# A sandwich layer with windowed attention on one core: q and k rows stored lane by head, loaded by half slots in 16 transfers, with signals per half slot

## The chip, the cores and the metric

The kernel runs on one core of a Trainium2 chip. The metric is the device time of one execution in microseconds (us), lower is better. TensorE, VectorE, ScalarE, GpSimd and SyncE are the engines of the core; SyncE (SP) does no arithmetic here, it issues DMA transfers one after the other from its queue, and 16 DMA engines carry them out.

## What is computed

x has 2 sequences of 2048 tokens with 128 features. The layer is, cut to what matters (all in float32, LN without gain):

```python
x = x + LN(attn(LN(x)))          # this part holds the change
x = x + LN(ffn(LN(x)))           # 4 experts, argmax routing, exact gelu; not touched

def attn(x):
    q, k, v = split(x @ qkv_w + qkv_b, 3)         # 16 heads of 8
    # head by head: position t sees positions t-128 .. t-1
    local = softmax(mask(q k^T / sqrt(8))) v
    # 64 pooled tokens per sequence, 4 heads of 8, earlier chunks only
    remote = (softmax(mask(rq rk^T / sqrt(8))) rv) @ rout_w + rout_b
    gate = sigmoid(local @ gl_w + remote_h @ gr_w)
    return (gate * local + (1 - gate) * remote_h) @ out_w + out_b
```

## The kernel before, in words

The work has three stages, each a block of programs for the five engines; all engines must have finished a stage before the next one begins: `project`, `attend` and `ffn`. The order on every engine is written out by hand (a function `emit` per engine, called for each chunk or step), and semaphores tie the engines together. A `Signal` is a semaphore with a count per step.

**project** runs over 8 chunks of 512 tokens. Per chunk: statistics and normalisation (VectorE, with GpSimd for the root), transposes (TensorE), copies (ScalarE, line 626), then the products q, k, v and rq (TensorE, lines 685 to 697). q and k are wanted at more than bfloat16 precision, so each is split in three bfloat16 parts whose sum it is: ScalarE writes the high part (line 633), VectorE the residue (line 527), ScalarE the middle part (line 643), GpSimd the low part (line 593). SyncE stores the parts to DRAM (`store`, lines 444 to 455): q_parts and k_parts, three transfers each, then v_tok and rq_t. The tiles `split`, `vt` and `rqs` have two buffers, so ScalarE's high part of chunk c waits on `s_out` for the stores of chunk c-2.

In DRAM q_parts and k_parts have the shape [part, chunk, d, head, token]. The partitions of the product are (head, d), and the store turns that round.

**The load.** In attention a product of q and k is one matmul over 48 rows: six of the nine products of parts, each over 8 rows d. Therefore `qst` holds the parts of q as row blocks 0,1,2 = part 0 three times, 3,4 = part 1 twice, 5 = part 2, and `kst` holds parts 0,1,2, then 0,1, then 0 of k. Both have two slots; a slot holds one chunk (4 blocks of 128 tokens, 16 heads). The slot is loaded in 4 groups of 4 heads, with three transfers for q and three for k in each (`load_q`, `load_k`, lines 222 to 237):

```python
RUNS = ((0, 3), (3, 2), (5, 1))
src = scratch[0][part, c, :, heads]...           # [8, 4 * 512]
sp.dma_start(dst, src.unsqueeze(0).broadcast_to([times, HD, HG * CH]))
src = scratch[1][0:parts, c, :, heads]...        # [parts, 8, 4 * 512]
```

`load_rest` adds vst (from v_tok) and rqT (from rq_t). All 26 transfers of a slot count on one semaphore, `s_load[slot]`.

**When the loads are issued.** Chunk 0 is loaded in `project`, by `first_blocks`: groups 0 and 1 behind the store of chunk 4, groups 2 and 3 with vst and rqT behind the store of chunk 5. Chunk 1 is loaded at the very start of `attend`. Chunk c from 2 on is loaded in steps 4(c-1) (q) and 4(c-1)+1 (k, then vst and rqT); `paced` holds SyncE until TensorE has got to a named unit of the transposed scores (`s_ST`), since the slot is still being read.

**attend** runs over steps s of one block of 128 tokens, with 8 units g of two heads per step. TensorE makes in unit g the scores of block s+2 (`scores`, lines 930 to 936), for VectorE to take the row maxima (line 1088), and the transposed scores of block s (`scores_t`, lines 948 to 967), for ScalarE's exponentials (line 1291), then products with v (line 981). The negated maxima of a block are split by GpSimd (line 1226), transposed by TensorE, copied by ScalarE (line 1303) to `mT` and written by a DMA (SyncE, line 895, "the maxima's transfer") into two further rows of `qst`; block s+1's go out in the middle of step s and `scores_t` of block s+1 waits for them. The wait for a slot stands on TensorE in front of unit 0 of the scores of its first block:

```python
if g == 0 and n.mod(LC) == 0:      # n = s + 2, in step s = 4c - 2
    pe.wait_ge(s_load[c % SLOTS], 16 * LOADS * (c // SLOTS + 1))
```

At its start `attend` has VectorE clear three PSUM banks and fill small tiles (lines 1072 to 1076), and TensorE waits for that (`s_consts`).

## Time and profile before

| what | us |
| --- | --- |
| median of 3 runs | 685.05 |
| lowest and highest run | 683.4 and 690.52 |
| the profiled execution | 687.44 |
| its span (first to last instruction) | 685.6 |
| project, until SyncE's first issue of attend | 94.2 |
| attend, until TensorE's last work in it | about 504 |

A profile shows one execution. "Busy" is time in which an engine worked on an instruction; a matmul's end is modelled. A wait is put down to what came last. PE is TensorE's matmuls, PEld its weight loads, DVE VectorE, ACT ScalarE, POOL GpSimd, SPq SyncE's queue. The clock is the share of full speed that TensorE was granted, 1.00 or 0.50 at any time. The DMA share is the mean busy share of the 16 DMA engines.

### The profile page before, as it was taken

How to read it: one execution, taken by the hardware profiler on the slowest of the kernel's cores; microseconds unless marked ns; L12 is line 12 of the kernel's file. 1: busy time of each engine (PE TensorE's matmuls, PEld its weight loads, DVE VectorE, ACT ScalarE, POOL GpSimd, SP SyncE). 2: the span in 40 equal slices, each digit the busy share in tenths (PEclk: the TensorE clock that was granted, in tenths of full speed). 3: DMA queues.
4: the chain of work that ended last, by engine and by line, in shares of the span. 5: the costliest groups of instructions: out<-in, count | busy, mean ns of one | idle time of the engine just before them, and what ended most of it. 6: DMA issues, size and time to landing. Idle time of an engine off the chain costs nothing. (4 is left out here: it accounts for less than half of the span.)

```text
span 685.6 us, 28265 instructions
## 1 busy us (share of the span) xinstructions
PE 558.6 (81%) x11345; PEld 391.0 (57%) x11345; DVE 407.7 (59%) x2034; ACT 288.9 (42%) x787; POOL 238.4 (35%) x465
## 2 busy tenths in 40 slices
PE   7887545979599598697685895898789999999992
PEld 3544212757477376475564674676536777667772
DVE  6684424557367386276464465477656467667655
ACT  2353200657367376276464464487512221221110
POOL 5545100134235243153243233245531243342342
PEclk9999867799799799599799698599999999999998
DMA  3474532111202102002002012000000000000001
GB/s 77 133 212 154 173 111 83 41 61 44 78 6 64 58 13 78 36 22 90 15 28 90 8 32 88 5 6 6 3 0 1 1 2 15 15 15 16 17 15 31
DMA packets 28506, 33.30 MB, mean 49 GB/s; under 512 B 5852, under 2 KB 22212, under 8 KB 28380
## 3 DMA queue, kind: packets, MB, share of 16 engines
q1 hardware_dynamic: 27324, 31.20, 14.6%
q8 instruction: 88, 1.44, 0.9%
q10 hardware_dynamic: 1056, 0.35, 0.2%
q14 instruction: 38, 0.31, 0.2%
HBM read 19.93 MB, written 11.27 MB: 46 GB/s over the span
## 5 line engine op out<-in xcount | busy, mean ns | idle before, releaser
L1088 DVE CUSTOM_DVE_ANT_0 added<-psS,maskq 128x160 bf16<-128x160 f32 x512 | 157.1, 316 | 147.6 <-PE psS L936 87.9
L1291 ACT ACTIVATE probs<-psST 128x512 f32<-128x512 f32 x256 | 152.7, 604 | 157.1 <-PE psST L967 154.3
L967 PE MATMUL psST<-qst,kst 98*32 98x128 bf16 (+3 forms) x2048 | 86.9, 207 | 5.6 <-issue 5.4
L981 PE MATMUL psPV<-probs,vst 128*9 128x128 f32 x1984 | 88.0, 289 | 2.2 <-issue 2.2
L963 PE MATMUL psST<-qst,kst 98*32 98x32 bf16 (+3 forms) x1920 | 83.6, 207 | 5.1 <-issue 5.0
L1263 POOL TENSOR_TENSOR gated<-both,glr 128x256 f32<-128x256 f32 x32 | 23.5, 733 | 143.0 <-DVE both L1189 143.0
L933 PE MATMUL psS<-kst,qst 68*32 68x96 bf16 (+3 forms) x512 | 24.3, 231 | 57.7 <-DMA rqT<-rq_t 48.8
L1724 ACT ACTIVATE hT<-fpsH 128x512 f32<-128x512 f32 x32 | 19.1, 598 | 121.6 <-PE fpsH L1468 121.6
L930 PE MATMUL psS<-kst,qst 68*32 68x160 bf16 x1536 | 67.0, 241 | 3.3 <-issue 2.3
L963 PEld LDWEIGHTS psST<-qst,kst 98*32 98x32 bf16 x1920 | 60.2, 101 | 6.5 <-issue 6.5
L951 PE MATMUL psST<-maskk,identb 128*32 128x128 bf16 x960 | 60.9, 231 | 0.3 <-issue 0.3
L967 PEld LDWEIGHTS psST<-qst,kst 98*32 98x32 bf16 x2048 | 55.9, 103 | 6.6 <-issue 6.3
L933 PEld LDWEIGHTS psS<-kst,qst 68*32 68x32 bf16 x512 | 14.8, 110 | 74.7 <-DMA rqT<-rq_t 50.5
L1465 PE MATMUL fpsH<-xehi,w1hi 128*128 128x512 f32 x128 | 55.7, 435 | 0.0
L981 PEld LDWEIGHTS psPV<-probs,vst 128*9 128x9 f32 x1984 | 49.9, 94 | 4.6 <-issue 3.2
L1465 PE MATMUL fpsH<-xelo,w1hi 128*128 128x512 f32 x128 | 50.6, 395 | 0.0
L1465 PE MATMUL fpsH<-xehi,w1lo 128*128 128x512 f32 x128 | 50.5, 395 | 0.0
L930 PEld LDWEIGHTS psS<-kst,qst 68*32 68x32 bf16 x1536 | 31.6, 96 | 30.7 <-issue 15.4
L1088 DVE DVE_READ_ACCUMULATOR2_ANT rowmax<- 128x1 f32 x512 | 42.1, 82 | 0.1
L1325 ACT ACTIVATE lexp<-psA,lbias 128x64 f32<-128x64 f32 x128 | 39.8, 328 | 0.0
L1644 DVE TENSOR_TENSOR xehi<-fpsE,xfThi 128x512 fp32r<-128x512 f32 x32 | 22.0, 688 | 17.5 <-PE fpsE L1476 9.7
L951 PEld LDWEIGHTS psST<-maskk,identb 128*32 128x32 bf16 x960 | 29.6, 101 | 4.4 <-ACT probs L1291 2.3
(183 smaller groups left out, 1237.7 us busy)
## 6 DMA issues: line engine op xcount, KB each, us to landing
q_parts<-split SPq DMA_DIRECT2D x24, 128.0 KB, 2.7
k_parts<-split SPq DMA_DIRECT2D x24, 128.0 KB, 2.7
qst<-q_parts SPq DMA_DIRECT2D x32, 96.0 KB
kst<-k_parts SPq DMA_DIRECT2D x32, 96.0 KB
v_tok<-vt SPq DMA_DIRECT2D x8, 288.0 KB, 2.6
vst<-v_tok SPq DMA_DIRECT2D x8, 288.0 KB
X<-in_L_attn_x_dram SPq DMA_DIRECT2D x8, 256.0 KB, 3.2
qst<-q_parts SPq DMA_DIRECT2D x32, 64.0 KB
```

The lines of the kernel that those rows point to most:

```text
L930: last = nc.tensor.matmul(bank[quad(i), a, 0:WIN], q, part(kst, KPROD, n - 1, h, QD * i, WIN), start=True, stop=True)
L933: nc.tensor.matmul(bank[quad(i), a, 0:P - QD * i], q, part(kst, KPROD, n - (1 if n.k else 0), h, QD * i, P - QD * i), start=True, stop=True)
L951: nc.tensor.matmul(bank[quad(j)].rearrange("p a (s q) -> p a s q", s=2)[:, :, :, quad(j)], pick, maskk[:].unsqueeze(1).broadcast_to([P, 2, ...
L963: nc.tensor.matmul(bank[quad(j), a, 0:QD * (j + 1)], part(kst, KALL, n - 1, h, QD * j, QD), part(qst, KALL, n, h, 0, QD * (j + 1)), start= ...
L967: last = nc.tensor.matmul(bank[quad(j), a, P + QD * j:2 * P], part(kst, KALL, n, h, QD * j, QD), part(qst, KALL, n, h, QD * j, P - QD * j) ...
L981: last = nc.tensor.matmul(psPV[32 * t:32 * t + VW, G * P:(G + 1) * P], vst[:, (n - 1 + side).mod(RING), 4 * G + t, :], probs[:, unit, (2 * ...
L1088: taken = nc.vector.tensor_tensor_reduce(added[:, h], psS[g % 2][:, a, 0:WIN], mask, 1.0, NEG * 4, ALU.add, ALU.max, rowmax[:, n.mod(2), h ...
L1263: nc.gpsimd.tensor_tensor(gated[:].rearrange("p h (a e) -> p a h e", a=2), both[:, n.mod(4)].rearrange("p a (h e) -> p a h e", h=H), glr[: ...
L1291: nc.scalar.activation(probs[:, g], psST[g % 2][:].rearrange("p a c -> p (a c)"), ACT.Exp, scale=SCALE).then_inc(s_exp.sem, 1)
L1325: nc.scalar.activation(lexp[:, h], psLS[:, h * NLAT:(h + 1) * NLAT], ACT.Exp, bias=lbias[:, s.mod(2), h:h + 1], scale=SCALE, accum_out=lsu ...
L1465: nc.tensor.matmul(psH[j % 2][:], w[:, e, tile], x[:, u, e], start=(e == 0 and k == 0), stop=False)
L1644: nc.vector.tensor_tensor(xehi[:, u, e], psE[e % 2][:], xfThi[:, u].bitcast(F32), ALU.mult)
```

## The change

Four things change.

1. *Lane by head.* ScalarE copies the q and k weights once into `wqk` with reordered columns, before chunk 0, and the biases are read in the same order; TensorE waits for the two copies (`s_lanes`). The partitions of the products are then (d, head), and the DRAM tensors become [chunk, part, (d, head), token]. The three parts of q are one store, and those of k another: 4 stores per chunk in place of 8.
2. *Fewer and larger loads.* A slot is loaded in two halves of 8 heads, each with three transfers for q and four for k, with vst and rqT: 16 in place of 26. The row of a head group is contiguous, 8 heads x 512 x 2 bytes = 8 KB, in place of 4 KB, and source and destination are plain matrices. In k the six blocks hold other parts (0, 1, 0, 1, 1, 2); with q's (0, 1, 2, 0, 1, 0) they give the same six products.
3. *Signals.* `s_half[half][slot]` replaces `s_load`: TensorE waits for half 0 in front of unit 0 and for half 1 in front of unit 4 of the scores, and for vst and rqT (`s_rest`) only two steps later, in front of `scores_t` of the first block. The wait for `s_consts` moves there too, in step 0.
4. *Places.* Chunk 1 is now loaded in `project` as well, behind the stores of chunks 6 and 7. In attention, step 4(c-1) issues half 0 (q at its start, k after unit 4 of the transposed scores), and the next step half 1 with vst and rqT.

```diff
-HG = 4
-STORES = 16 * 8
-LOADS = 6 * H // HG + 2
-RUNS = ((0, 3), (3, 2), (5, 1))
+HALF = H // 2
+STORES = 16 * 4
+RUNS_Q = ((0, 0, 3), (3, 0, 2), (5, 0, 1))
+RUNS_K = ((0, 0, 1), (1, 0, 1), (2, 0, 2), (4, 1, 2))
+LOADS = 16 * (len(RUNS_Q) + len(RUNS_K))
...
+def load_half(sp, c, half, side, held, scratch, s_half):
+
+    u, heads = c % SLOTS, slice(half * HALF, (half + 1) * HALF)
+    tile, runs = ((held.qst, RUNS_Q), (held.kst, RUNS_K))[side]
+    rows = scratch[side][c].rearrange("a (d h) t -> (a d) h t", h=H)[:, heads].rearrange("r h t -> r (h t)")
+    for first, part, parts in runs:
+        sp.dma_start(tile[first * HD:(first + parts) * HD, u, heads].rearrange("r h t -> r (h t)"),
+                     rows[part * HD:(part + parts) * HD]).then_inc(s_half[half][u], 16)
...
-        q_parts = nc.dram_tensor("q_parts", [3, NCH, HD, H, CH], BF16, kind="Internal").ap()
+        q_parts = nc.dram_tensor("q_parts", [NCH, 3, P, CH], BF16, kind="Internal").ap()
...
-                    for part in range(3):
-                        sp.dma_start(parts[part, c.k].rearrange("d h t -> h d t"),
-                                     split[:, u, side, part]).then_inc(s_out[u], 16)
+                    sp.dma_start(parts[c.k].rearrange("a p t -> p a t"), split[:, u, side]).then_inc(s_out[u], 16)
...
-                for hg in range(2 * k, 2 * k + 2) if k < 2 else ():
-                    load_q(sp, 0, hg, held, scratch, s_load)
-                    load_k(sp, 0, hg, held, scratch, s_load)
-                if k == 1:
-                    load_rest(sp, 0, held, scratch, s_load)
+                for side in range(2):
+                    load_half(sp, k // 2, k % 2, side, held, scratch, s_half)
+                if k % 2:
+                    load_rest(sp, k // 2, held, scratch, s_rest)
...
+            for side in range(2):
+                nc.scalar.activation(wqk[:, side].rearrange("k (d h) -> k d h", h=H),
+                                     wqkv[:, side * D:(side + 1) * D].rearrange("k (h d) -> k d h", h=H),
+                                     ACT.Copy).then_inc(s_lanes, 1)
...
+                half = s.mod(LC) if s.live and 2 <= c < NCH and s.mod(LC) < 2 else None
+                if half is not None:
+                    sp.wait_ge(s_ST.sem, s_ST.after(s - 1))
+                    load_half(sp, c, half, 0, held, scratch, s_half)
...
+                if half is not None:
+                    if half == 0:
+                        sp.wait_ge(s_ST.sem, s_ST.after(s, HALF // 2))
+                    load_half(sp, c, half, 1, held, scratch, s_half)
+                if half == 1:
                     sp.wait_ge(s_pv.sem, s_pv.after(s - 1))
-                    paced(s, 5)
-                    load_rest(sp, c, held, scratch, s_load)
+                    load_rest(sp, c, held, scratch, s_rest)
...
-            pe.wait_ge(s_consts, CONSTS)
...
-                        if g == 0 and n.mod(LC) == 0:
+                        if g % (HALF // 2) == 0 and n.mod(LC) == 0:
                             c = n.k // LC
-                            pe.wait_ge(s_load[c % SLOTS], 16 * LOADS * (c // SLOTS + 1))
+                            pe.wait_ge(s_half[2 * g // HALF][c % SLOTS], LOADS * (c // SLOTS + 1))
```

SyncE's queue at the end of `project`, before: the stores of chunk 7 (and the last of chunk 6's), the end of the stage, and the first issues of `attend`. An operand such as 24x1x2048 is the shape of the transfer, x2 a repetition.

```order
L451 DMA v_tok<-vt 128x576 [waits s_vt]
L455 DMA rq_t<-rqs 32x512 [waits s_rqs]
L479 DMA kst<-ones 2x16x512 [waits s_clear_late]
L479 DMA kst<-ones 2x16x512
L448 DMA q_parts<-split 16x8x512 [waits s_lo]
L448 DMA q_parts<-split 16x8x512 x2
L448 DMA k_parts<-split 16x8x512 [waits s_lo]
L448 DMA k_parts<-split 16x8x512 x2
L451 DMA v_tok<-vt 128x576 [waits s_vt]
L455 DMA rq_t<-rqs 32x512 [waits s_rqs]
L317 UNCONDITIONAL_BRANCH [waits s_out1,s_out0,s_ones]
L869 UNCONDITIONAL_BRANCH [waits barrier_Pool_Activation_PE_DVE_SP_release]
```

The same place now, from the stores of chunk 7 on: its loads of chunk 1's second half stand between the stores and the end of the stage.

```order
L443 DMA q_parts<-split 128x3x512 [waits s_lo]
L443 DMA k_parts<-split 128x3x512 [waits s_lo]
L445 DMA v_tok<-vt 128x576 [waits s_vt]
L449 DMA rq_t<-rqs 32x512 [waits s_rqs]
L229 DMA qst<-q_parts 24x4096
L229 DMA qst<-q_parts 16x4096
L229 DMA qst<-q_parts 8x4096
L229 DMA kst<-k_parts 8x4096 x2
L229 DMA kst<-k_parts 16x4096 x2
L237 DMA vst<-v_tok 128x576
L239 DMA rqT<-rq_t 32x512
L311 UNCONDITIONAL_BRANCH [waits s_out1,s_out0,s_ones]
```

The stage ends behind 16 issues less of stores (4 per chunk over chunks 4 to 7) and 6 more of loads.

SyncE's queue in attention, steps 4 and the start of 5 (chunk 2), before; `qst<-mT` is the maxima's transfer.

```order
L895 DMA qst<-mT 2x16x128 [waits s_mTc]
L228 DMA qst<-q_parts 24x1x2048 [waits s_ST]
L228 DMA qst<-q_parts 16x1x2048
L228 DMA qst<-q_parts 8x2048
L228 DMA qst<-q_parts 24x1x2048
L228 DMA qst<-q_parts 16x1x2048
L228 DMA qst<-q_parts 8x2048
L895 DMA qst<-mT 2x16x128 [waits s_mTc]
L228 DMA qst<-q_parts 24x1x2048 [waits s_ST]
L228 DMA qst<-q_parts 16x1x2048
L228 DMA qst<-q_parts 8x2048
```

The same steps now, with the start of step 5:

```order
L878 DMA qst<-mT 2x16x128 [waits s_mTc]
L229 DMA qst<-q_parts 24x4096 [waits s_ST]
L229 DMA qst<-q_parts 16x4096
L229 DMA qst<-q_parts 8x4096
L878 DMA qst<-mT 2x16x128 [waits s_mTc]
L229 DMA kst<-k_parts 8x4096 [waits s_ST]
L229 DMA kst<-k_parts 8x4096
L229 DMA kst<-k_parts 16x4096 x2
L229 DMA qst<-q_parts 24x4096 [waits s_ST]
L229 DMA qst<-q_parts 16x4096
L229 DMA qst<-q_parts 8x4096
L878 DMA qst<-mT 2x16x128 [waits s_mTc]
```

In step 4 stand now 3 issues of q and 4 of k where 12 of q stood; k no longer waits for step 5, and q's second half does.

## Rows read from the trace of the kernel before

**Rows 1.** The page: span, busy time by engine, and granted clock and DMA in 40 slices

```profile
span 685.6 us, 28265 instructions
...
PE 558.6 (81%) x11345; PEld 391.0 (57%) x11345; DVE 407.7 (59%) x2034; ACT 288.9 (42%) x787; POOL 238.4 (35%) x465
...
PEclk9999867799799799599799698599999999999998
DMA  3474532111202102002002012000000000000001
```

**Rows 2.** The list of waits: engine and line, who was waited for, total us, times, longest

```profile
ACT probs L1291 <- PE psST L967: 154.3, 130, 11.7
...
PE psS L933 <- DMA rqT<-rq_t: 48.8, 6, 8.8
...
ACT split L633 <- DMA rq_t<-rqs: 17.5, 5, 7.0
...
PE psST L948 <- DMA qst<-mT: 8.2, 1, 8.2
```

**Rows 3.** The timeline of SyncE's queue, 206 to 227 us: start, us, what, count

```profile
206.59 3.78 SPq L228 DMA_DIRECT2D qst<-q_parts  x6
...
221.56 3.75 SPq L237 DMA_DIRECT2D kst<-k_parts  x6
225.42 0.36 SPq L244 DMA_DIRECT2D vst<-v_tok  x1
225.82 0.42 SPq L246 DMA_DIRECT2D rqT<-rq_t  x1
```

**Rows 4.** Stretches of the DMA tail: us, busy times, clock, DMA share, GB/s

```profile
226.00:228.00 2.00, 0.00 (x0) 0.00 (x0) 0.27 (x3) 0.00 (x0) 0.66 (x3) 1.00 0.71 214
228.00:232.00 4.00, 0.00 (x0) 0.00 (x0) 0.00 (x0) 0.00 (x0) 0.00 (x0) 0.59 0.14 53
```

**Rows 5.** Stretches between every fourth copy of the maxima: first, last, and the sum of six

```profile
142.80:191.20 48.40, 37.84 (x1284) 28.80 (x1283) 27.84 (x181) 27.55 (x85) 17.23 (x43) 0.89 0.17 52
...
383.60:435.00 51.40, 40.12 (x1286) 30.26 (x1285) 28.54 (x184) 28.20 (x86) 17.61 (x44) 0.80 0.13 42
sum 292.20, PE 226.89 PEld 173.92 DVE 168.74 ACT 166.56 POOL 105.41; mean PE 37.82 PEld 28.99 DVE 28.12 ACT 27.76 POOL 17.57
```

**Rows 6.** Single steps as stretches, and one fall of the clock

```profile
174.10:177.50 3.40, 3.40 (x77) 2.19 (x69) 1.76 (x11) 1.55 (x6) 0.00 (x0) 0.50 0.22 77
201.30:209.80 8.50, 8.47 (x307) 6.60 (x305) 6.86 (x46) 6.78 (x23) 3.41 (x10) 1.00 0.08 21
435.00:447.40 12.40, 12.40 (x349) 9.31 (x347) 6.70 (x46) 7.10 (x23) 3.55 (x9) 0.65 0.01 3
```

**Rows 7.** The timeline at the start of attention: VectorE, ScalarE, TensorE

```profile
95.56 0.48 DVE L1072 MEMSET psPV<- 128x512 f32 x1 [11.09 <-issue]
...
98.12 0.32 DVE L1088 CUSTOM_DVE_ANT_0 added<-psS,maskq 128x160 bf16<-128x160 f32 x1 [0.74 <-PE psS L936]
...
109.36 0.27 ACT L1303 ACTIVATE mT<-psB 32x128 bf16<-32x128 bf16 x1 [32.00 <-PE psB L1016]
...
120.59 0.41 PE L948 MATMUL psST<-never,identb 128*32 128x256 bf16 x4 [8.22 <-DMA qst<-mT]
```

**Rows 8.** The timeline of SyncE's queue at the end of the projection stage

```profile
51.71 1.85 SPq L448 DMA_DIRECT2D q_parts<-split  x3
...
56.74 2.25 SPq L228 DMA_DIRECT2D qst<-q_parts  x3
...
89.88 0.38 SPq L455 DMA_DIRECT2D rq_t<-rqs  x1
```

**Rows 9.** The timeline of ScalarE and TensorE in the projection stage

```profile
12.98 0.60 ACT L626 ACTIVATE xnT<-psT 128x512 f32<-128x512 f32 x1 [6.55 <-PE psT L674]
...
73.76 0.69 ACT L633 ACTIVATE split<-psQ,bq 128x512 bf16<-128x512 f32 x1 [6.99 <-DMA rq_t<-rqs]
...
82.95 5.57 PE L122 MATMUL psW<-filler 128*128 128x512 bf16 x25
```

More of the change, by code:

```diff
@@ L219, in apply, with load_rest @@
         last.then_inc(self.s_xf.sem, 1)
[L222 to L240 removed]
+def load_half(sp, c, half, side, held, scratch, s_half):
[5 more added lines that the diff above has]
+                     rows[part * HD:(part + parts) * HD]).then_inc(s_half[half][u], 16)
+def load_rest(sp, c, held, scratch, s_rest):
     _, _, v_tok, rq_t = scratch
@@ L276, in sandwich @@
         norm = InputNorm(nc, sb, lambda name: ctx.enter_context(nc.semaphore(name)), X, eps_col, mhalf)
-        s_load = [ctx.enter_context(nc.semaphore(f"s_load{r}")) for r in range(SLOTS)]
+        s_half = [[ctx.enter_context(nc.semaphore(f"s_half{j}{r}")) for r in range(SLOTS)] for j in range(2)]
+        s_rest = [ctx.enter_context(nc.semaphore(f"s_rest{r}")) for r in range(SLOTS)]
         until_attend = ctx.enter_context(ExitStack())
@@ L397, in project @@
         s_prep = sem("s_prep")
+        s_lanes = sem("s_lanes")
         s_lat = sem("s_lat")
@@ L667, in _ @@
             pe.wait_ge(s_w, all_weights)
+            pe.wait_ge(s_lanes, 2)
             def transpose(c):
```

70 lines of the change are left out of this document (19 added, 51 removed).

## The prediction

> **What bounds the kernel now.** I read four views, in this order. The page first [rows 1]: over the whole span TensorE is busy 81%, more than any other engine, yet in the middle slices (the attention stage) the row of granted clock falls from 9 to 7 or less at regular distances. The DMA engines are busy 1 or 2 tenths there, so their bandwidth as a whole is not used up.
>
> The list of waits says why [rows 2]. TensorE waited six times, 48.8 us in all, for the last transfer of the next slot's load (rqT) and once 8.2 us for the row of maxima (qst from mT). ScalarE waited 17.5 us in five pieces for stores in the projection stage. ScalarE's long wait (154 us) is a wait for the matmuls: it shows that TensorE leads, and costs nothing.
>
> Third, SyncE and the DMA engines at one of the six places [rows 3, 4]. SyncE issues the 24 q and k transfers of a slot at 0.62 us each (3.75 us for six), the last at 225.8 us, and TensorE has stood still since 225.5 us, because it waits for the whole slot at the first unit of step 4c-2. After the last issue the DMA engines are busy 0.14 of 16, that is 2.2 engines, at 53 GB/s, until the load has landed at about 233.7 us. Two engines hold a queue and fourteen are empty. One of the two moves 53/2.2 = 24 GB/s, so a 4 KB row takes about 0.17 us.
>
> Fourth, the stretches [rows 5, 6]. I cut the trace at every fourth copy of the maxima (ScalarE's line 1303). Six such periods of four blocks take 292.2 us with TensorE busy 226.9 us. A step of one block in a quiet place at full clock takes 8.50 us, busy 8.47: there TensorE alone sets the pace.
>
> **The load.** How the rows fall on engines is my reading of the operands. A slot has 8 groups (4 head groups, q and k) of three transfers. The sources count 3 copies or parts, then 2, then 8 rows in front. If that front count is the number of engines used, the two lowest engines get 8 + 8 + 1 = 17 rows of 4 KB per group, 136 of the slot's 384; at 0.17 us that is 23 us. This agrees with two engines still busy 8 us after SyncE's last issue, with the first issue at 206.6 us [rows 3, 4]. The Trainium skill, "DMA: Bandwidth & Descriptors", section "Why a DMA increments its semaphore by 16 and not by 1", says it directly: the engines used are the largest number up to 16 that divides the slowest dimension (not 1) of source and destination, taken from the lowest. By that rule the trace agrees, at 2.2 engines.
>
> After the change a transfer is a plain matrix of 24, 16 or 8 rows of 8 KB. If all rows count, the busiest engine gets 2 + 1 + 1 rows of q and 1 + 1 + 1 + 1 of k per half, 16 rows per slot, 16 x 0.34 = 5.4 us in place of 23. If instead they stay on two engines, half the bytes are about 23 us again; both ends are kept, and I take the first, as the 2.2 engines fit that reading and no other I can think of.
>
> The time at which they are needed moves too. The q half and the k half of heads 8 to 15 are issued in step 4c-3 (7 issues, at most 0.62 us each, 4.3 us), and needed at the fifth unit of step 4c-2; vst and rqT are needed two blocks later than before. That is over 8.5 us after the issue [rows 6]: the six waits go, 48.8 us.
>
> **The clock.** After each stall the granted clock is at its lower level (1.2 GHz in place of 2.4) while work goes on. A step mostly at the lower level has 349 matmuls in 12.40 us, the quiet one 307 in 8.50 [rows 6]. With a mean clock of 0.65, 8.7 us of it are at the half level and 3.7 at the full one; those 3.7 take 134 matmuls at 28 ns, which leaves 215 in 8.7 us, 40 ns each: 0.3 of such time is lost. From the mean clocks of the six periods (0.89, 0.90, 0.90, 0.81, 0.91, 0.80) 77 us are at the half level [rows 5]; The clock falls some 3.3 us into a stall (228 to 232 us has a mean of 0.59, so it fell at 228.7 [rows 4]), so 48.8 - 6 x 3.3 = 29 of the 77 lie in the stalls themselves and 48 in work: 15 us lost. So a period's matmul work at full clock is (226.9 - 15)/6 = 35.3 us, and its idle time beside the stall (292.2 - 226.9 - 48.8)/6 = 2.75: 38.0 us. I put 0.6 on top for clock falls that follow no stall. 6 x 38.6 = 231.6: **60.6 us gained**, stalls and clock together. If the clock did not recover it would be 12 less, if it never fell 4 more. The step after the sixth period takes 12.4 us; its 349 matmuls at 28 ns are 9.8, with 0.3 idle 10.1 [rows 6]: **2.3**.
>
> **Start of attention.** Now slot 1 is loaded there: 26 issues are 16 us of SyncE's queue, from 94.2 to 110.7, and keep the two engines until about 120. The maxima of block 0 were copied at 109.36, and their transfer (2 rows in front, so the same two engines) lands at 120.5 [rows 7]: **8.2 us gained**, as these loads are issued before. The half clock behind it costs less afterwards, **1.5**. That TensorE no longer waits for the memsets gives the first unit of scores, 0.7 us (VectorE's first maximum waited 0.74 [rows 7]): **0.7**, since VectorE's own start does not move.
>
> **Projection stage.** From 51.7 us SyncE issues without a gap: four groups of stores (8 issues, 5.0 us each), 12 loads (7.9), 14 loads (8.8), two rows of ones (1.4), and gaps: 38.5 us until 90.26 [rows 8]. Then it waits for the last store (2.6) and all engines leave the stage: it is the last, TensorE had ended at 88.5 [rows 9]. Afterwards a store group is 4 issues, 0.62 + 0.62 + 0.6 + 0.37 = 2.2 us; the loads are 7 + 9 + 7 + 9 issues, although 16 of them are new here. A two-dimensional transfer costs 0.36 (vst) or 0.42 (rqT), a three-dimensional one 0.62 [rows 3]; I take 0.44 for 28 of them and 0.8 for each pair of vst and rqT: 14. Sum 8.8 + 14 + 1.4 = 24 us (at 0.62: 29). The last stores are followed by 9 loads, so their landing is covered. ScalarE's high parts waited five times, 17.5 us, for stores of two chunks before [rows 2]; the last one, chunk 7's, 6.99 us, was chunk 5's store behind 12 load issues [rows 8, 9]. From high part to landed store I count 10.5 to 11.5 us per two chunks, so chunk 7's comes at about 59.5 us in place of 73.8, and TensorE's end 14.7 us behind it, at 74.2. SyncE's chain, begun at 48, ends at 72 to 77. The stage ends at about 75.9 in place of 92.9: **17.0 us gained**. Lower bound 9 (issue time alone, at 0.62), upper bound 19.
>
> Added: two copies of 128 x 128 on ScalarE before chunk 0. ScalarE sat idle 6.55 us before its first copy, at 12.98 us, while TensorE ran fillers [rows 9]: nothing, with that cover gone 0.6 us. The reordered bias is 128 runs of 4 bytes, as before. The feed-forward stage (190 us) is not touched.
>
> **Sum.** 60.6 + 2.3 + 8.2 + 1.5 + 0.7 + 17.0 = 90.3 us. The profiled execution took 687.4 (span 685.6 and 1.8 around it): 597.1. It lay 2.4 above the median of the runs (685.05): **595 us**.
>
> **Rivals.**
> - The clock stays as it is. For it: the trace has falls of the clock that no stall precedes, as at 174.1 us [rows 6]. Then the 15 us are not won back, and the projection gives 13 instead of 17: 595 + 14 + 4 = 613.
> - The rows still gather on two engines (a front count is not what decides). The slot's 23 us fit into a period of 38, so the long wait still goes, but each of 12 steps with loads has the maxima's transfer behind 8 KB rows on those two engines, 2 to 4 us late: 36 us. About 631. Against it: nothing else explains 2.2 engines.
> - Slower: plain matrices land on one engine. 192 rows of 8 KB at 0.34 us are 65 us per slot. From 38.6 us per slot on, the load sets the period, and at 48.7 the gain is gone; at 65 the six periods take 98 us more than before, about 685 - 28 + 98 = 755. Against it: when vst and rqT, plain matrices too, are under way, the share of busy engines is 0.71, at 214 GB/s [rows 4].
> - The loads moved into the projection are what ends it: 32 loads at 0.62 us and stores that wait for them, the stage ends at 84: 603. That is inside the range.
>
> Chances: forecast 0.64, clock 0.2, two engines 0.09, the longer projection 0.05, one engine 0.02. The range takes in the bounds of projection and clock: 580 (2 better in the projection, periods of 37.5 us, and 3 us at the start of attention if the clock is up there) to 618. Faster by over 1%, which is about what a measurement of this kernel can tell from no change: 0.97; within 1%: 0.01; slower: 0.02.
>
> **What the profile after would show.** The wait for rqT is gone, and none of over 1 us for a half slot stands in its place. Periods of four blocks take 38 to 39 us, with a clock over 0.95. After SyncE's last issue of a slot the DMA share falls within 2 or 3 us, not 8. TensorE's wait for the maxima at the start of attention is under 1 us. VectorE's memset of psPV starts at 77 to 80 us in place of 95.56. The prediction is wrong if the periods stay over 42 us with gaps on TensorE, if SyncE is at the stage's end after 84 us, or if load issues cost over 0.62 us.

## The result, and the profile after

| what | before, us | after, us |
| --- | --- | --- |
| median of 4 runs each | 684.64 | 637.99 |
| lowest and highest run | 683.4 and 690.52 | 630.17 and 643.61 |
| the profiled execution | 687.44 | 643.61 |
| its span | 685.6 | 641.8 |

The ratio is 0.9265, 95% interval 0.9159 to 0.937: the change made the kernel 47 us faster, where 90 were forecast (595 us, range 580 to 618). The profiled execution is the longest and slowest of the four runs, 5.6 us above their median, so what is read from its trace is too long by up to as much.

One slip in the section on the change: the six row blocks of k hold the parts (0, 0, 0, 1, 1, 2), as `RUNS_K` in the diff says, and not (0, 1, 0, 1, 1, 2). No time hangs on it.

The page after:

```profile
span 641.8 us, 28150 instructions
...
PE 556.4 (87%) x11337; PEld 391.6 (61%) x11345; DVE 407.5 (63%) x2034; ACT 290.3 (45%) x789; POOL 238.1 (37%) x465
...
PEclk9898959889796999996988987998999999999997
DMA  3478930214212224043032142000000000000001
...
q1 hardware_dynamic: 25788, 31.20, 21.0%
q8 instruction: 88, 1.44, 1.0%
```

Beside [rows 1] TensorE's busy time is almost the same (558.6 before), so nearly all of the gain is idle time that went. The clock row still has holes, and the middle slices of the DMA row are higher. q1 carries the data, q8 is a queue of its own that brings instructions: 88 packets, 1.44 MB, 16 KB each. The prediction did not count with it.

TensorE's waits within the six periods, copies of the maxima 4 to 28 (engine, line, what ended the wait, total us, times, longest):

```profile
PE psST L940 <- issue: 9.3, 7, 1.8
PE psST L944 <- issue: 8.8, 6, 3.4
PE psPV L958 <- issue: 5.0, 6, 2.1
PE psST L928 <- issue: 4.7, 3, 1.9
```

The six waits for rqT of [rows 2] (48.8 us) are gone, and no wait for a half slot stands here. What stands here ends with "issue", with nothing that the profile can name: 22 pauses and 27.8 us in these four rows, 32.3 us with the smaller ones, of 35.0 us of idle time. The same sum is 15.4 us in the six periods of the kernel before.

The six periods, and the step after them, as stretches (us, then busy of PE, PEld, DVE, ACT, POOL, clock, DMA share, GB/s):

```profile
125.90:171.30 45.40, 40.65 (x1288) 30.79 (x1286) 27.38 (x178) 27.72 (x85) 16.46 (x42) 0.85 0.29 55
...
347.10:391.80 44.70, 38.25 (x1288) 29.35 (x1286) 28.86 (x185) 27.80 (x86) 17.52 (x44) 0.91 0.28 48
sum 265.90, PE 230.94 PEld 177.59 DVE 168.56 ACT 166.74 POOL 105.27; mean PE 38.49 PEld 29.60 DVE 28.09 ACT 27.79 POOL 17.54
...
391.80:403.10 11.30, 11.30 (x347) 8.51 (x345) 6.61 (x44) 7.14 (x23) 3.56 (x10) 0.70 0.03 5
```

Against [rows 5] the six take 265.9 us in place of 292.2: TensorE's idle time falls from 65.3 to 35.0 us, but its busy time rises from 226.9 to 230.9. The clock is 0.90 on average, not over 0.95: by its records TensorE was at the lower level for 54.8 us of the six periods (76.6 before). Every fall there stands behind a pause of TensorE of 0.9 us or more.

The start of attention, on VectorE, ScalarE and TensorE, against [rows 7]:

```profile
88.81 0.48 DVE L1054 MEMSET psPV<- 128x512 f32 x1 [14.35 <-issue]
...
90.86 0.33 DVE L1070 CUSTOM_DVE_ANT_0 added<-psS,maskq 128x160 bf16<-128x160 f32 x1 [0.23 <-DVE psST L1058]
...
101.56 0.27 ACT L1285 ACTIVATE mT<-psB 32x128 bf16<-32x128 bf16 x1 [31.46 <-PE psB L998]
...
104.48 0.29 PE L925 MATMUL psST<-never,identb 128*32 128x256 bf16 x4
```

The first transposed scores follow the copy of the maxima by 2.9 us (11.2 before), without a wait for their transfer. But the memset that opens the stage comes at 88.81, not at 78.5. The end of the projection stage says why, first SyncE's queue, then stretches:

```profile
74.14 0.90 SPq L449 DMA_DIRECT2D rq_t<-rqs  x1
75.08 1.45 SPq L229 DMA_DIRECT2D qst<-q_parts  x3
76.58 1.46 SPq L229 DMA_DIRECT2D kst<-k_parts  x4
...
78.54 0.43 SPq L239 DMA_DIRECT2D rqT<-rq_t  x1
```

```profile
76.00:78.00 2.00, 2.00 (x10) 0.94 (x10) 0.00 (x0) 0.00 (x0) 0.00 (x0) 1.00 1.09 286
...
80.00:82.00 2.00, 0.00 (x0) 0.00 (x0) 0.00 (x0) 0.00 (x0) 0.00 (x0) 0.93 1.12 198
82.00:84.00 2.00, 0.00 (x0) 0.00 (x0) 0.00 (x0) 0.00 (x0) 0.00 (x0) 0.50 0.72 138
84.00:86.00 2.00, 0.00 (x0) 0.00 (x0) 0.00 (x0) 0.00 (x0) 0.00 (x0) 0.50 0.54 164
```

SyncE has issued all at 78.97 us, 2 us after the forecast's 72 to 77, and then waits 7.9 us for the last store (rq_t). All 16 DMA engines are full until 82 (a share over 1 is overlap in the records) and still have work at 86; TensorE does nothing from 78.5 to 89.1 us. So the stage waits for bytes, not for issues.

Where the 43.8 us between the two profiled executions come from, by the terms of the prediction:

| term | forecast | measured |
| --- | --- | --- |
| six periods | 60.6 | 26.3 |
| projection, until the memset of psPV | 17.0 | 6.75 |
| from there to the fourth copy of the maxima | 10.4 | 10.2 |
| from the 28th copy to TensorE's last matmul in attention | 2.3 | 0.8 |
| sum | 90.3 | 44.0 |

### The profile page after: what moved, and what is told of

The parts are those of the page before. It is cut to its first block and busy times, and to the rows that moved or that the text cites. A ratio compares the mean times of both kernels' runs of the same rounds, so it can differ in the third digit from the quotient of the medians.

```text
span 641.8 us, 28150 instructions
## 1 busy us (share of the span) xinstructions
PE 556.4 (87%) x11337; PEld 391.6 (61%) x11345; DVE 407.5 (63%) x2034; ACT 290.3 (45%) x789; POOL 238.1 (37%) x465
## 3 DMA queue, kind: packets, MB, share of 16 engines
q1 hardware_dynamic: 25788, 31.20, 21.0%
q8 instruction: 88, 1.44, 1.0%
## 5 line engine op out<-in xcount | busy, mean ns | idle before, releaser
L944 PE MATMUL psST<-qst,kst 98*32 98x64 bf16 (+3 forms) x2048 | 86.6, 206 | 9.2 <-issue 9.1
L958 PE MATMUL psPV<-probs,vst 128*9 128x128 f32 x1984 | 90.0, 292 | 5.0 <-issue 5.0
L928 PE MATMUL psST<-maskk,identb 128*32 128x128 bf16 x960 | 62.2, 234 | 5.8 <-issue 4.7
L907 PEld LDWEIGHTS psS<-kst,qst 68*32 68x32 bf16 x1536 | 30.8, 97 | 33.0 <-issue 17.3
L910 PE MATMUL psS<-kst,qst 68*32 68x96 bf16 (+3 forms) x512 | 23.0, 217 | 10.9 <-issue 10.9
L1447 PEld LDWEIGHTS fpsH<-xehi,w1hi 128*128 128x128 f32 x128 | 24.0, 188 | 11.9 <-issue 8.4
```

What stands on the lines that cost most here:

```text
L907: last = nc.tensor.matmul(bank[quad(i), a, 0:WIN], q, part(kst, KPROD, n - 1, h, QD * i, WIN), start=True, stop=True)
L910: nc.tensor.matmul(bank[quad(i), a, 0:P - QD * i], q, part(kst, KPROD, n - (1 if n.k else 0), h, QD * i, P - QD * i), start=True, stop=True)
L928: nc.tensor.matmul(bank[quad(j)].rearrange("p a (s q) -> p a s q", s=2)[:, :, :, quad(j)], pick, maskk[:].unsqueeze(1).broadcast_to([P, 2, ...
L944: last = nc.tensor.matmul(bank[quad(j), a, P + QD * j:2 * P], part(kst, KALL, n, h, QD * j, QD), part(qst, KALL, n, h, QD * j, P - QD * j) ...
L958: last = nc.tensor.matmul(psPV[32 * t:32 * t + VW, G * P:(G + 1) * P], vst[:, (n - 1 + side).mod(RING), 4 * G + t, :], probs[:, unit, (2 * ...
L1447: nc.tensor.matmul(psH[j % 2][:], w[:, e, tile], x[:, u, e], start=(e == 0 and k == 0), stop=False)
```

## What the pauses are

In a trace read instruction by instruction, the pauses of TensorE have a pattern that no view prints. I counted TensorE's instructions (matmuls, weight loads, and the waits and other instructions of its sequencer) in the order of their records and cut them into pieces of 256. The number of the instruction that follows a pause of 0.6 us or more in the six periods, less a fixed offset, modulo 256:

```
before     0 or 1 (13 pauses, 0.6 to 1.2 us); 165, 210, 255, 172, 217, 6 (the waits for rqT)
after      0, 1 or 2 (23 of 23 pauses, 0.6 to 3.4 us)
a_noload   0, 1 or 2 (17 of 17 pauses, 0.7 to 1.8 us; an experiment, below)
```

So every pause of this length that is no wait for data stands at a cut. In the kernel after it ends 1.3 to 1.9 us after the end of a packet on q8, and a packet of 16 KB for 256 instructions is 64 bytes for each. A packet starts on average 1.30 us after TensorE has crossed the cut before, and takes 1.25 (without loads 1.13 and 1.13). With 1.4 us from its end to the next instruction that is some 3.9 us for 256 instructions (3.7 without loads). TensorE crosses a cut every 3.88 us in the middle (median of a_noload; some come after 2.8): it has almost no slack against the arrival of its own program, and had little before the change either.

Two of these pauses of the kernel after, with the load issues before them (TensorE, SyncE, then stretches):

```profile
154.72 0.23 PE L940 MATMUL psST<-qst,kst 98*32 98x96 bf16 x2 [1.36 <-issue]
...
368.82 0.24 PE L944 MATMUL psST<-qst,kst 98*32 98x96 bf16 x3 [3.39 <-issue]
```

```profile
148.50 1.42 SPq L229 DMA_DIRECT2D kst<-k_parts  x4
...
363.05 1.05 SPq L229 DMA_DIRECT2D qst<-q_parts  x3
```

```profile
145.00:147.00 2.00, 2.00 (x79) 1.73 (x78) 1.60 (x12) 1.80 (x4) 1.70 (x6) 1.00 0.83 127
...
149.00:151.00 2.00, 1.38 (x38) 0.97 (x38) 0.80 (x6) 0.29 (x2) 0.00 (x0) 1.00 0.80 164
...
153.00:155.00 2.00, 0.64 (x36) 0.49 (x39) 1.61 (x10) 0.74 (x3) 1.38 (x4) 1.00 0.00 0
...
363.00:365.00 2.00, 2.00 (x98) 1.65 (x94) 2.00 (x15) 1.87 (x6) 1.23 (x5) 1.00 0.67 135
365.00:367.00 2.00, 0.43 (x29) 0.28 (x22) 1.40 (x10) 0.28 (x1) 1.70 (x5) 1.00 0.45 66
367.00:369.00 2.00, 0.18 (x4) 0.18 (x3) 0.00 (x0) 0.00 (x0) 0.16 (x1) 0.86 0.03 4
```

A burst of loads occupies 13 of 16 engines (share 0.83) at 127 GB/s; TensorE pauses some microseconds later, when the DMA engines are idle again (0.00, 0.03) and nothing is being waited for. From this I formed the theory that the experiments test: **the load rows, now on nearly all engines, hold up the packets that bring TensorE its instructions; it pauses at the next cut, and the clock falls to its lower level for a while.** The rivals: the pauses are TensorE's waits for the half slots, put down wrongly; or they belong to the instruction stream alone and would be there without loads.

The Trainium skill, "Runtime: NRT & Kernel Launch", section "Instruction fetch mechanics", says that an engine fetches its program in blocks of 16 KiB, 256 instructions, over a DMA queue of its own, and calls the cost mostly hidden. The blocks and the queue are in this trace; hidden they are not: 32.3 us of pauses in 265.9.

## The experiments

Each ran beside the kernel before on the same chip. "Six" is the sum of the six periods in the profiled execution, "busy" and "idle" TensorE's in it; ratios are to the kernel before.

| kernel | median, us | ratio, 95% | six | busy | idle |
| --- | --- | --- | --- | --- | --- |
| after | 637.99 | 0.9265 (0.9159 to 0.937) | 265.9 | 230.9 | 35.0 |
| a_noload | 612.13 | 0.8923 (0.8869 to 0.8978) | 234.9 | 213.2 | 21.7 |
| b_dump | 632.85 | 0.92 (0.9123 to 0.9277) | 258.0 | 224.0 | 34.0 |
| a_two | 656.53 | 0.9587 (0.9515 to 0.9659) | 258.6 | 229.6 | 29.0 |
| a_whole | 640.7 | 0.9291 (0.9217 to 0.9365) | 267.7 | 229.8 | 37.9 |
| a_attend | 635.39 | 0.9265 (0.9208 to 0.9322) | 265.1 | 228.6 | 36.5 |
| a_wide | 623.65 | 0.9059 (0.9017 to 0.91) | 250.0 | 219.6 | 30.4 |
| a_eight | 624.57 | 0.9079 (0.903 to 0.9128) | 254.2 | 221.4 | 32.8 |
| a_quarter | 620.02 | 0.9009 (0.8967 to 0.905) | 247.6 | 220.5 | 27.1 |
| a_paced | 626.52 | 0.9086 (0.9038 to 0.9133) | 246.7 | 217.6 | 29.1 |
| b_qa | 611.62 | 0.891 (0.8853 to 0.8967) | 245.9 | 223.0 | 22.9 |
| b_qp | 622.63 | 0.9077 (0.9017 to 0.9137) | 248.6 | 222.8 | 25.8 |
| b_qap | 620.49 | 0.9035 (0.8982 to 0.9088) | 246.1 | 219.2 | 26.9 |

"Six", "busy" and "idle" come from one execution each. The kernel after and a_attend have the same loads in attention and almost the same six periods, 265.9 and 265.1 us, though a_attend's execution took 8.8 us less.

**No loads in attention (a_noload).** TensorE waits only for the first load of each slot, and blocks 8 to 31 are computed from the rows of chunks 0 and 1.

```diff
-                half = s.mod(LC) if s.live and 2 <= c < NCH and s.mod(LC) < 2 else None
+                half = None
...
-                            pe.wait_ge(s_half[2 * g // HALF][c % SLOTS], LOADS * (c // SLOTS + 1))
+                            pe.wait_ge(s_half[2 * g // HALF][c % SLOTS], LOADS)
...
-                            pe.wait_ge(s_rest[c % SLOTS], 16 * 2 * (c // SLOTS + 1))
+                            pe.wait_ge(s_rest[c % SLOTS], 16 * 2)
```

> The changed kernel without the slot loads of chunks 2 to 7 in attention (and without their three waits), so those blocks are computed from the data of chunks 0 and 1. Theory 1 (instruction supply): in the trace of the changed kernel every pause of TensorE put down to issue ends about 1.4 us behind a 16 KB instruction packet, and the long ones lie where load rows hold the DMA engines. Then these long pauses go, but the floor of about 3.9 us per instruction block stays: six periods of four blocks take 246 to 252 us in place of 266, time about 621. Theory 2 (clock and dependences, loads have no part in it): 634 to 642 as the changed kernel. The forecast's own picture (only the loads keep a period from 38.6 us): six periods in 232, time about 603.

Measured: 612.13 us. Two periods and the sum of the six:

```profile
124.50:164.40 39.90, 38.54 (x1287) 29.43 (x1286) 27.39 (x180) 27.54 (x86) 16.66 (x42) 0.88 0.06 14
164.40:203.20 38.80, 34.86 (x1285) 27.09 (x1284) 28.45 (x184) 27.68 (x86) 17.65 (x45) 1.00 0.02 6
...
sum 234.90, PE 213.20 PEld 165.14 DVE 168.19 ACT 165.66 POOL 105.07; mean PE 35.53 PEld 27.52 DVE 28.03 ACT 27.61 POOL 17.51
```

The floor is lower than I then thought, and almost what the prediction had computed: 39.15 us a period in place of 38.6, with 35.5 of matmul work in place of 35.3, at a clock of 1.00 in four of the six periods. So the prediction's arithmetic of a period was right for a kernel whose loads cost nothing, and the loads cost 31.0 us in these two executions (25.9 in the medians): 13.3 of idle time and 17.7 of longer matmuls. The matmuls are longer by the clock, which was at its lower level for 13.2 us here and 54.8 in the kernel after. Where it stays at 1.00, loads make no difference to them: the last period of a_paced, with loads, has TensorE busy 35.33 us, and the last one here 35.09.

**The same traffic into a tile that nobody reads (b_dump).** As a_noload, but with the loads of q and k.

```diff
+        dump = sb("dump", [6 * HD, 2, HALF, CH], BF16)
...
+                sp.dma_start(dump[first * HD:(first + parts) * HD, side].rearrange("r h t -> r (h t)"),
+                             rows[part * HD:(part + parts) * HD]).then_inc(s_dump, 16)
...
-                    load_half(sp, c, half, 0, held, scratch, s_half)
+                    load_dump(sp, c, half, 0)
```

> No step waits for a load, but the traffic stays: the q and k transfers of chunks 2 to 7 go, with the same shapes and at the same places, into a tile that nobody reads (vst and rqT of those chunks are left out, and blocks 8 to 31 are computed from the rows of chunks 0 and 1). Theory 1 (the load rows hold up the transfers that bring TensorE its instructions, so traffic alone costs the time): the six periods take about 258 to 266 us as with the real loads, and the time is 630 to 638 us. Theory 2 (what costs time is that TensorE depends on the loads, by its waits for the halves): the time is that of the kernel without loads, about 612 us, with periods of 235 us in sum.

```profile
sum 258.00, PE 223.98 PEld 172.87 DVE 169.17 ACT 166.84 POOL 105.35; mean PE 37.33 PEld 28.81 DVE 28.19 ACT 27.81 POOL 17.56
```

Measured: 632.85 us, and the six periods are at 258.0. Nothing on TensorE depends on these transfers, yet 23.1 of the 31.0 us are there (20.7 of 25.9 in the medians), and the waits put down to "issue" are 29.3 us, against 16.8 without loads and 32.3 in the kernel after. The traffic costs the time, not the waits. The other 8 us are left between the missing vst and rqT, the waits for them, and the scatter of single executions.

**All of a slot awaited at its first unit (a_whole).** The change's signals for the loads undone; the wait for `s_consts` stays where the change put it.

```diff
-                            pe.wait_ge(s_half[2 * g // HALF][c % SLOTS], LOADS * (c // SLOTS + 1))
+                            for j in range(2):
+                                pe.wait_ge(s_half[j][c % SLOTS], LOADS * (c // SLOTS + 1))
+                            pe.wait_ge(s_rest[c % SLOTS], 16 * 2 * (c // SLOTS + 1))
```

> The changed kernel with the half signals undone: TensorE waits for both halves and for vst and rqT in front of the first unit of a slot. If the spread loads land within 3 us of their last issue (theory of the forecast), no wait over 1 us stands there and the time is that of the changed kernel, 634 to 642. Rival (the half signals are what removed the wait): waits of 2 to 5 us at six places, 650 to 665.

```profile
PE psS L910 <- DMA rqT<-rq_t: 10.9, 4, 3.2
```

Measured: 640.7 us. The wait for rqT is back, four times and 10.9 us, in place of six times and 48.8 [rows 2]. I had expected none over 1 us. The six periods grow by only 1.8 us; that such a wait for data covers a pause that the program's arrival would have caused anyway is not shown. The signals per half are worth too little to tell from the scatter; the larger and better spread transfers took the long waits away.

**Rows gathered on two engines (a_two).** Each part plane gets 16 rows of padding in DRAM, so that parts and rows stay two dimensions, and a transfer has 3 or 2 in front.

```diff
-        q_parts = nc.dram_tensor("q_parts", [NCH, 3, P, CH], BF16, kind="Internal").ap()
+        q_parts = nc.dram_tensor("q_parts", [NCH, 3, P + H, CH], BF16, kind="Internal").ap()
...
-                     rows[part * HD:(part + parts) * HD]).then_inc(s_half[half][u], 16)
+                     rows[part:part + parts]).then_inc(s_half[half][u], 16)
```

> The changed kernel with part planes set apart in DRAM, so that the 24-row and 16-row loads keep 3 and 2 in front, as before the change. Bytes, row length, places and signals are those of the changed kernel. If the front count sets the number of DMA engines, the share after a slot's last issue is again about 0.13 for 10 us and more. Theory 1: the instruction packets mostly find free engines, the long issue pauses go, periods take 41 to 43 us in place of 44.4; but the projection stage ends later than 87 us, since stores queue behind loads on two engines; sum 625 to 640. Rival: the maxima's transfers, which go through the same two engines, are late in the 12 load steps: periods over 46 us and a wait for the maxima on TensorE of 10 us or more in all.

Its waits, and a stretch of a load:

```profile
PE psST L928 <- DMA qst<-mT: 17.9, 7, 4.1
...
PE psST L940 <- issue: 5.7, 6, 2.7
PE psST L944 <- issue: 3.4, 5, 0.9
```

```profile
164.00:166.00 2.00, 2.00 (x50) 1.35 (x44) 1.59 (x12) 1.67 (x4) 1.70 (x6) 1.00 0.24 78
```

Measured: 656.53 us. The share of busy engines in a load is 0.24 where it was 0.83, so the count in front of a transfer does decide how many engines carry it. The time is over the 625 to 640 us of the first theory, since what the rival names, late maxima, came on top. The psPV memset comes at 108.32 us, and the maxima's transfer is awaited seven times, 17.9 us. But the pauses of the kind "issue" shrink (in the six periods from 32.3 to 9.7 us), and the six periods are 7.3 us shorter than with all engines. An 8 KB row takes 311 ns here (median of the records) and 643 ns in the kernel after.

**Chunk 1 at the start of attention (a_attend).** The place of the loads undone, with 16 issues in place of 26.

```diff
-                for side in range(2):
-                    load_half(sp, k // 2, k % 2, side, held, scratch, s_half)
+                for side in range(2) if k < 2 else ():
+                    load_half(sp, 0, k % 2, side, held, scratch, s_half)
...
+            for half in range(2):
+                for side in range(2):
+                    load_half(sp, 1, half, side, held, scratch, s_half)
+            load_rest(sp, 1, held, scratch, s_rest)
```

> The changed kernel with chunk 1 loaded at the start of attention again (16 issues). Theory: in the changed kernel the end of the projection stage is set by the last stores, which queue behind 8 KB rows of chunk 1 on all 16 DMA engines (SyncE waited 7.9 us for them). Then VectorE's first memset of attention comes at 80 to 83 us in place of 88.8, the maxima's first transfer is not late (under 1 us of wait on TensorE), and the time is 630 to 633. Rival: the backlog only moves into attention: the transfer of block 0's maxima waits again 3 us or more and the time stays at 636 to 640.

VectorE, and the wait for the maxima on TensorE:

```profile
77.96 0.48 DVE L1059 MEMSET psPV<- 128x512 f32 x1 [5.94 <-issue]
...
95.29 0.41 PE L930 MATMUL psST<-never,identb 128*32 128x256 bf16 x4 [3.95 <-DMA qst<-mT]
```

Measured: 635.39 us. The memset comes at 77.96, within the 77 to 80 that the prediction named: the 17 us of the projection are there as soon as chunk 1's loads are not. Of the 10.9 us gained at the memset 8.5 are left at the fourth copy of the maxima (117.37 against 125.87), as part is paid back in a wait of 3.95 us for the maxima. The ratio is the same as the kernel after's, 0.9265: in the medians the gain is 2.6 us, less than their scatter. So the earlier end of the stage is shown, a shorter kernel by it is not; of the two expectations the rival, a wait of 3 us or more for the maxima, came nearer.

**Other shapes of the same bytes.** a_wide: one transfer of 48 rows per half and side, into every second partition (0 to 94), so that the products are made of other rows than the reference's. a_eight: every transfer has 8 rows, 12 per half. a_quarter: every transfer cut in two of 4 heads, 28 per slot with rows of 4 KB. a_paced: one transfer per unit of the transposed scores instead of three or four in a row.

```diff
# a_wide
+        sp.dma_start(tile[0:96:2, u, heads].rearrange("r h t -> r (h t)"),
+                     rows).then_inc(s_half[half][u], 16)
# a_eight
-RUNS_Q = ((0, 0, 3), (3, 0, 2), (5, 0, 1))
-RUNS_K = ((0, 0, 1), (1, 0, 1), (2, 0, 2), (4, 1, 2))
+RUNS_Q = tuple((i, part, 1) for i, part in enumerate((0, 1, 2, 0, 1, 0)))
+RUNS_K = tuple((i, part, 1) for i, part in enumerate((0, 0, 0, 1, 1, 2)))
# a_quarter
+    for heads in (slice((2 * half + j) * 4, (2 * half + j + 1) * 4) for j in range(2)):
...
# a_paced
+                    load_half(sp, c, half, 0, held, scratch, s_half,
+                              lambda i: sp.wait_ge(s_ST.sem, s_ST.after(s, i)) if i else None)
...
```

> The changed kernel with other loads for chunks 2 to 7 in attention: per half and side one transfer of 48 rows of 8 KB into every second partition from 0 to 94, in place of rows gathered in partitions 0 to 47. Bytes and row length are the same; those chunks are computed from wrong rows. Without loads six periods took 234.9 us, with them 265.9. Theory 1a (rows from 8 to 16 engines crowd into few partitions, so each row holds its engine twice as long, 9.6 GB/s per engine in place of 24, and TensorE's instruction packets wait behind them): the rate in a load's stretch rises from about 130 GB/s at a share of 0.83 to over 220 GB/s, the long pauses shrink, periods take 40.5 to 42 us in place of 44.3, time 618 to 626. Theory 1b (any burst on all engines delays the packets, whatever the rows' rate): 43.5 to 45, time as the changed kernel.

> The changed kernel with every q and k load as a transfer of one block, 8 rows of 8 KB: 12 in a half in place of 7. By the front count they use 8 engines. Theory 1: if the instruction packets run on an engine outside the lowest eight, the long pauses go and periods take 40 to 42 us; if inside, or if the rows' slow writing is what counts, 44 to 46. At the projection's end 10 issues more per pair of halves: VectorE's first memset of attention 90 to 95 us. Sum 625 to 645.

> The changed kernel with each transfer cut in two of 4 heads, rows of 4 KB (28 in place of 14 per slot), same engines, bytes and signals. Theory 1 with packets: an instruction packet waits behind whole rows on its engine, so half the row, half the wait: pauses from late packets (fetch start over 2 us behind the last one) from 6 to 2 or fewer, periods 42 to 43 us. Rival (it is the burst's length that counts, not the row): 44 to 45. The projection's end is as in the changed kernel, within 3 us, since the same bytes stand there.

> The changed kernel with the loads of attention spread over a step: one transfer per unit (q's three at units 0, 1, 2, k's four at units 4 to 7), in place of three and four in one burst. Same rows, bytes and engines. Theory 1: each burst is 0.5 to 1.5 us in place of 2 to 4, so no instruction packet waits over 1.5 us; the pauses over 1.5 us (14.6 us over six periods) go, and with them most falls of the clock: periods 41 to 42.5 us, time 620 to 630. Rival: the delay is spread over more packets and the sum stays: 44 us, 636 to 640.

Measured: 623.65, 624.57, 620.02 and 626.52 us. All four are faster than the kernel after, with intervals clear of its own, but not of one another. a_quarter has the lowest median, with its six periods at

```profile
sum 247.60, PE 220.51 PEld 170.79 DVE 168.79 ACT 166.11 POOL 105.02; mean PE 36.75 PEld 28.47 DVE 28.13 ACT 27.68 POOL 17.50
```

More issues and smaller rows win over fewer and larger ones. The late packets did not become 2 or fewer, as a_quarter's expectation has it, but 4. What the traces' records say of the load rows and of the instruction blocks in the six periods:

```
            load rows           all rows    mean us per     blocks whose packet
            KB   median ns      together    256 instr.      began over 2 us after the cut
a_noload     -       -              0 us       3.88               0
a_two        8     311            440          4.27               7
a_wide       8     348            528          4.13               7
a_quarter    4     219            555          4.09               4
a_paced      8     495            622          4.07               2
a_eight      8     707            777          4.20              11
after        8     643            795          4.39               6
b_dump       8     644            806          4.26               6
```

"All rows together" is the time that load rows held a DMA engine, summed over engines. Leaving out a_two, whose maxima wait as well, the sum of the six periods follows it only roughly: 234.9, 250.0, 247.6, 246.7, 254.2, 265.9, 258.0. The three with the least stand below the three with the most, but within each three it orders nothing. The same bytes take between 440 and 806 us of the engines, and one row takes longer where more of them are under way in few partitions. The Trainium skill, "SBUF — State Buffer", section "Door 1: The DMA port swizzle", states that groups of four partitions share one of 16 ports and that bit 6 of the partition number picks the other half of them. a_wide, whose rows go over partitions 0 to 94 and so to more ports by that rule, agrees: 348 ns a row against 643, and 304 GB/s at a share of 0.87 (159.1 to 161.1 us) against 127 at 0.83. But a_wide also has one transfer where the kernel after has three or four, so the partitions are not shown to be the cause. The count of late packets (a packet more or less hangs on where the cut is set) orders these kernels worse than the time that the rows take (a_wide 7 of them, a_paced 2).

**Together (b_qa, b_qp, b_qap).** 4 KB rows with chunk 1 at the start of attention; 4 KB rows paced over the units; all three. The edits are those above.

> 4 KB rows (28 transfers per slot) and chunk 1 loaded at the start of attention instead of in the projection stage. Theory 1 (rows that hold an engine for a shorter time delay the instruction fetch less; and the projection stage ends 10 us earlier): the two gains add, psPV is cleared at 78 us, the copy of the 28th maxima comes at about 361 us, and the time is 612 to 616 us. Rival (the loads at the start of attention collide with the maxima's transfer and the fetches there, as far as they don't in the projection): 619 to 624 us, with a wait for the maxima of over 4 us at the start.

> 4 KB rows, and one run of rows (two transfers) per unit of the transposed scores instead of all at once. Theory 1 (shorter rows and smaller bursts both leave the fetch more room): six periods of 240 to 245 us, 612 to 618 us. Rival (each alone has taken what there is, the rest of the gap to the kernel without loads is the bandwidth that the rows take in any order): six periods of 246 to 249 us, 619 to 623 us.

> All three: 4 KB rows, paced over the units, chunk 1 at the start of attention. Theory 1 (all add): 605 to 612 us. Rival (the pieces overlap): not faster than the better of the two pairs, 614 to 621 us.

Measured: 611.62, 622.63 and 620.49 us. b_qa, VectorE at the start of attention, TensorE's wait there, and the six periods:

```profile
80.50 0.48 DVE L1060 MEMSET psPV<- 128x512 f32 x1 [5.97 <-issue]
...
96.38 0.29 PE L931 MATMUL psST<-never,identb 128*32 128x256 bf16 x4 [1.22 <-DMA qst<-mT]
```

```profile
sum 245.90, PE 222.95 PEld 171.62 DVE 168.31 ACT 166.46 POOL 105.22; mean PE 37.16 PEld 28.60 DVE 28.05 ACT 27.74 POOL 17.54
```

With short rows the move to attention pays: the wait for the maxima is 1.22 us in place of 3.95, and **b_qa is the fastest kernel of the study**, ratio 0.891 (0.8853 to 0.8967). Against a_quarter (0.9009, to 0.8967 at its lower end) the gain is 8.4 us in the medians, with intervals that touch. Pacing on top adds nothing (b_qp 622.63 against a_quarter's 620.02), and b_qap, 620.49, lies 8.9 above b_qa. The traces do not put this down to the paced loads: the six periods are the same (246.1 against 245.9, and b_qp 248.6 against 247.6), and most or all of what the profiled executions of b_qap and b_qp have more (5.4 and 4.7 us) is there at the fourth copy of the maxima, before any paced load (124.05 against 118.42 us, and 126.23 against 122.19). VectorE's psPV memset is already late by 2.9 and 4.1 us, and a_paced has it at 93.46 where a_quarter has 87.99. Why was not followed up.

## Why the prediction was wrong

The direction was right and the size was not. By its own steps:

- *What bounds the kernel, and the load.* Right. The wait for rqT was for a load that sat on two engines; with plain matrices the engines in use went from 2.2 to 13, and a_two, with 3 and 2 in front again, went back to a share of 0.24, some 4 of 16. The six waits went.
- *The clock: "a period's matmul work at full clock is 35.3 us", "38.0 us", "I put 0.6 on top".* **This is the step that failed, by 34 of the missing 46 us.** Not the arithmetic: without loads it is 39.15 us (a_noload). What failed is the silent premise that loads off the critical path cost nothing once no engine waits for them: the six periods took 265.9 us in place of 231.6. The prediction counted the loads as issues and as landings, and never asked who else uses the DMA engines. TensorE's instructions do, on a queue whose row the page shows (q8), with next to no slack. Before the change fourteen engines were empty during a load [rows 4] and it showed little (15.4 us of pauses put down to "issue", 32.3 after); spreading the load over all engines is what made it dear, for a_two, back on few, has 9.7. b_dump shows the cost of the traffic with no wait for a load. That it reaches TensorE by way of the packets is read from the traces: the pauses stand at the cuts.
- *The rival "the clock stays as it is".* It came near the mark in the periods (15 us not won back; 17.7 measured between after and a_noload) but for another reason, and it lacked the 13.3 us of new idle time. Its 613 was 25 us too low. It was argued from a fall of the clock at 174.1 us that "no stall precedes"; the trace of before has a pause there, at one of the cuts, in front of this matmul:

```profile
172.19 0.22 PE L967 MATMUL psST<-qst,kst 98*32 98x96 bf16 x3 [1.16 <-issue]
```

The other fall of this kind, at 406.2 us, has one of 1.19 us that ends at 404.72. The arrival of the program stood in the trace that the prediction was made from. The 0.6 us per period put on top for such falls were its only term for this. The prediction also prices a clock that does not recover at 12, 15 and 14 us in three places, and gives no working for the 4 us that this rival takes from the projection.
- *The rival of two engines.* Rightly set aside: 656.53 us when it was made so, against 631 forecast for it. The late maxima cost 17.9 us and not 36, and the projection's end at 108 us was missing there. The rival of one engine did not come about either: a load has 13 of them.
- *Start of attention.* Right: 10.2 of 10.4.
- *Projection: "The last stores are followed by 9 loads, so their landing is covered".* **The second step that failed, by 10 us.** The issues took what was said (three q loads in 1.21 to 1.45 us, so 0.40 to 0.48 each; SyncE's last at 78.97). But the 9 loads do not cover the stores' landing, they delay it: the last store, issued at 74.14, shares all engines with 1.6 MB of load rows (192 of 8 KB, issued from 69.64 us on), at 138 to 286 GB/s, and the memset of psPV came at 88.81 us. a_attend, without the loads of chunk 1 there, has it at 77.96. The bound from below, 9 us, was taken from issue time alone and was too high for the 6.75 measured. The rival of the longer projection had the place right and the reason not: it counted issues at 0.62 us and an end at 84.
- *Added copies.* Right: ScalarE's first xnT copy at 13.08 in place of 12.98 us [rows 9].
- *The signals per half.* Listed with the load as what takes the waits away; a_whole, without them, is 2.7 us longer in the medians, within the scatter.
- *The signs of being wrong.* Two of the three came: periods of 44.3 us with gaps on TensorE, and SyncE at the stage's end until about 86.9 us. The load issues were not dearer.

What stays open: which of the DMA engines carries a given instruction packet, why a packet starts late in one burst and not in another, and why a_eight, whose rows are as slow as the kernel after's, is 13 us faster. The delay is read from the records, and shown by experiment only as the sum: traffic on, traffic off. That shorter rows help by leaving the packets more room is argued from the row times, not shown by itself.

## What to carry to other kernels

Before spreading or enlarging a background load, look whether an engine with a dense instruction stream has slack against its own program: pauses that end with "issue" at a fixed distance in instructions, beside a row of the instruction queue, say that it has none. Then a load has a price even if nobody waits for it, and its shape is worth trying: the same bytes in 4 KB rows, which hold the DMA engines for less time, took 18 us off here, in spite of twice the issues. And transfers put around a stage's last store delay that store: what can be loaded after the stage's end may be cheaper there. It was with 4 KB rows (b_qa, 8.4 us, with intervals that touch), and made no clear difference with 8 KB rows (a_attend).

## What was unexpected of the hardware

- TensorE's program arrives in pieces of 256 instructions, a 16 KB packet each, about as fast as this kernel uses them up, and its pauses of 0.6 us or more fall on the cuts. What is put down to "issue" is 32.3 us of 265.9 in the kernel after, and still 16.8 us of 234.9 with no loads at all.
- The time of one 8 KB row depends on its company: 311 ns with few engines busy, 643 to 707 with most, 348 in one transfer into a wider spread of partitions. The same 31.20 MB took 21.0% of the engines' span; in the form with 4 KB rows 18.0% of a shorter one.
- A load at a DMA share of 0.83 moved 127 GB/s and one at 0.80 moved 164, that is 9.6 to 12.8 GB/s for each busy engine, where the two lone engines of before moved 24 each [rows 4]. Thirteen engines in place of two were worth a factor of 2.4 to 3.1 in rate, not 6.
